# A decoder layer on one core: four score groups in one call over four banks, head and norm passes moved between engines, and the orders rewritten

## What is computed

```
x = layernorm(x + attn(x));  x = layernorm(x + wkv(x, ctx));  x = layernorm(x + ffn(x))

attn: q = rope(rms_norm(x@Wq.T + bq)) * gain     16 heads of 16 channels
      k = rope(rms_norm(x@Wk.T + bk)), v = x@Wv.T + bv      4 key heads, each shared by 4 query heads
      softmax(q k^T / 4, causal) v, then @Wo.T + bo
wkv:  num_t = exp(u + k_t) v_t + sum_{i<t} exp(k_i - (t-1-i) e^decay) v_i, den likewise without v, num / den
      with k = x and v = ctx, per channel
ffn:  (relu(x @ sign(up).T * up_s) @ sign(down).T) * down_s * out_s
```

## Time and profile before

| | |
|---|---|
| median of 3 runs | 215.16 us (214.39 to 215.67) |
| the profiled execution's own time | 215.18 us |
| its span, first to last instruction | 213.4 us |
| PE busy | 177.3 us (83%) |
| DVE busy | 177.4 us (83%) |
| ACT busy | 134.7 us (63%) |
| POOL busy | 114.2 us (54%) |
| mean granted TensorE clock | 0.964 |

### The profile page before, as it was taken

One profiled execution on the slowest core, in us unless ns is written; L12 is line 12 of the kernel. 1 busy time (PEld: TensorE's weight loads), 2 busy tenths in 40 slices (PEclk: granted clock), 3 DMA queues, 4 the chain that ended last, 5 costly groups with the idle time before them and its releaser, 6 DMA issues. The chain is left out here.

```text
span 213.4 us, 3906 instructions
## 1 busy us (share of the span) xinstructions
PE 177.3 (83%) x1240; PEld 106.4 (50%) x1240; DVE 177.4 (83%) x368; ACT 134.7 (63%) x250; POOL 114.2 (54%) x157
## 2 busy tenths in 40 slices
PE   1953897999999989999897999999799368689950
PEld 0432223354535745675375755746567347467740
DVE  2792555697996999999999999999999998998543
ACT  0443479957967789397478685778837329447820
POOL 7383247084176057835696369567255455376361
PEclk9999769999999999999999999999999999789995
DMA  6283915016600080033000530541010010010111
GB/s 216 51 309 134 260 61 123 5 27 136 185 0 2 3 221 0 3 66 108 5 0 0 120 104 0 146 129 49 2 54 0 0 49 3 2 49 0 52 52 52
DMA packets 19196, 14.81 MB, mean 69 GB/s; under 512 B 14307, under 2 KB 14563, under 8 KB 18918
## 3 DMA queue, kind: packets, MB, share of 16 engines
q1 hardware_dynamic: 18448, 14.43, 23.4%
q10 hardware_dynamic: 726, 0.11, 0.3%
HBM read 9.29 MB, written 2.10 MB: 53 GB/s over the span
## 5 line engine op out<-in xcount | busy, mean ns | idle before, releaser
L462 PE MATMUL banks<-dn_sb,hid_hi 128*128 128x256 bf16 x128 | 30.8, 281 | 8.2 <-DVE r L1517 4.7
L956 ACT ACTIVATE hid<-banks,ups_man 128x256 f32<-128x256 f32 x64 | 26.7, 473 | 14.9 <-PE banks L449 14.6
L903 ACT ACTIVATE probs<-banks 128x1024 f32<-128x1024 f32 x32 | 32.4, 1023 | 5.2 <-PE banks L359 5.0
L313 PE MATMUL banks<-wqkv_sb,xT_sb 128*128 128x384 f32 x64 | 26.4, 563 | 10.8 <-issue 6.2
L449 PE MATMUL banks<-x2hi,up_sb 128*128 128x256 f16 x128 | 29.6, 274 | 1.6 <-ACT hid L956 1.3
L462 PE MATMUL banks<-dn_sb,hid_lo 128*128 128x256 bf16 x128 | 30.7, 280 | 0.0
L449 PE MATMUL banks<-x2lo,up_sb 128*128 128x256 f16 x128 | 29.5, 273 | 0.0
L1226 POOL TENSOR_TENSOR newt<-ratio,rec 128x512 f32<-128x512 f32 x8 | 13.4, 1680 | 25.0 <-ACT rec L942 25.0
L313 PEld LDWEIGHTS banks<-wqkv_sb,xT_sb 128*128 128x128 f32 x64 | 13.1, 214 | 20.7 <-issue 13.1
L352 PE MATMUL banks<-rows 32*128 32x512 f16 x128 | 19.8, 386 | 2.6 <-ACT probs L903 1.2
L1594 DVE TENSOR_TENSOR hid_lo<-hid,hid_hi 128x512 f16<-128x512 f32 x24 | 19.0, 797 | 1.3 <-PE banks L462 1.1
(11 more groups left out here) (110 smaller groups left out, 382.3 us busy)
## 6 DMA issues: line engine op xcount, KB each, us to landing
xT_sb<-xT_dram SPq DMA_DIRECT2D x8, 256.0 KB, 3.2
x_sb<-x_dram SPq DMA_DIRECT2D x8, 256.0 KB, 3.3
ctxT_sb<-ctxT_dram SPq DMA_DIRECT2D x8, 256.0 KB, 3.5
out_dram<-outb SPq DMA_DIRECT2D x8, 256.0 KB, 2.2
up_f<-up_dram SPq DMA_DIRECT2D x1, 1024.0 KB, 4.9
dn_f<-down_dram SPq DMA_DIRECT2D x1, 1024.0 KB, 6.9
wqkv_sb<-wqkv_dram SPq DMA_DIRECT2D x1, 384.0 KB, 3.3
wo_sb<-wo_dram SPq DMA_DIRECT2D x1, 256.0 KB, 3.7
```

The lines of the kernel that those rows point to most:

```text
L313: nc.tensor.matmul(banks[:, PJ + t, 0:E], xT_sb[:, p % 2, c, t, :], wqkv_sb[:, c, :], start=(c == 0), stop=False)
L462: mm = nc.tensor.matmul(banks[:, DN, t * D:(t + 1) * D], part[:, j, t * S:(t + 1) * S], dn_sb[:, j, :], start=(j == 0 and t == 0 and m == ...
L903: nc.scalar.activation(probs[:, KVH * (m // 2) + m % 2:KVH * (m // 2) + m % 2 + 3:2].rearrange("p n j s -> p n (j s)"), banks[:, SC[m]:SC[ ...
L956: nc.scalar.activation(hid[:, j, :], banks[:, UP[n], (j % 2) * T * S:(j % 2 + 1) * T * S], ACT.Relu, scale=ups_man[:, j:j + 1]).then_inc(s ...
```

## The change

It has five parts.

1. `scores(p, t)` makes all four groups of a sequence in one call, over banks 6, 7, 2 and 3. The mask is added by products of 32 rows and 128 columns, four to a group. Half as many calls; `exps` still takes two banks at a time.
2. The banks are given out anew. Both products of a pair (`PV = (3, 2)`) share banks with the second half of a score call.
3. `normed(0, p)` and `normed(2, p)` run on ScalarE, as x * rstd + offset; GpSimd makes `less` = -mean and `offset` = less * rstd on two columns.
4. `scale_heads` and `keys_by_context` move from GpSimd to VectorE, with `newton_rms(1)`, `den_by_rec` of pairs 6 and 7 and `add_out` of pairs 0 and 7. `rope_sum` of pairs 1 to 7, `rope_sines(0)` and `rope_cosines(1)` move from VectorE to GpSimd, and of the 32 `low_bits` GpSimd has 16 (8 before).
5. The lists of TensorE, ScalarE, GpSimd and VectorE are in a new order; TensorE begins with seven products of zeros (`keep_busy`), and `project(2)` stands ahead of the branch. SP's list is the same.

```
-        PJ, AC, WO, X1, ZT, X2, DN = 2, 5, 0, 4, 2, 5, 0
-        PV = (1, 5)
-        UP = (5, 5, 0, 3)
-        SC = (6, 0, 6, 6)
+        PJ, AC, WO, X1, ZT, X2, DN = 4, 1, 1, 0, 4, 4, 1
+        PV = (3, 2)
+        UP = (4, 5, 3, 5)
+        SC = (6, 2, 6, 2)
+        NEWTON_ON_DVE = (1, )
...
+            def keep_busy(n):
+                pe.wait_ge(idle_ready, 1)
+                for k in range(n):
+                    nc.tensor.matmul(banks[:, X1], idle_b[:, 0:128], idle_b[:], start=True, stop=True)
...
+            def scores(p, t, guarded):
                 q = rows[:, p % 2]
                 landed(pe, "rows_in", p)
                 for k, kb in enumerate((HB * t + REP, T * HB + t)):
+                    for b in range(2):
+                        for s in range(2):
+                            r = VW * (b + 2 * s)
+                            nc.tensor.matmul(banks[:, SC[2 * t + b] + s], q[r:r + VW, kb, :],
+                                             q[r:r + VW, HB * t:HB * t + REP, :].rearrange("p j s -> p (j s)"),
+                                             start=(k == 0), stop=False)
+                for h in range(S // VW):
+                    for b in range(2):
+                        for s in range(2):
+                            r = VW * (b + 2 * s)
+                            mm[b][s] = nc.tensor.matmul(banks[:, SC[2 * t + b] + s]
+                                                        .rearrange("p (j s) -> p j s", j=REP)
+                                                        [:, :, h * VW:(h + 1) * VW],
+                                                        later[r:r + VW, h, :], masked[r:r + VW],
+                                                        start=False, stop=(h == S // VW - 1 and not guarded))
...
                 scores(0, 0, guarded)
-                scores(0, 1, guarded)
-                pe.wait_ge(sems["probs_done"], 1)
-                scores(0, 2, guarded)
                 pe.wait_ge(sems["probs_done"], 2)
+                scores(0, 1, guarded)
+                pe.wait_ge(sems["probs_done"], 4)
                 products(0, 0)
-                pe.wait_ge(sems["probs_done"], 3)
-                scores(0, 3, guarded)
+                pe.wait_ge(sems["probs_done"], 4)
+                products(0, 1)
...
+            def normed(n, p, rows_of, to, name):            # ScalarE
+                done(act, f"of{n + 1}", p)
...
+                for t in range(T):
+                    nc.scalar.activation(to[:, t], rows_of[:, t, :], ACT.Identity, bias=offset[n][:, t:t + 1],
+                                         scale=rstd[n][:, t:t + 1]).then_inc(sems[name], 1)
...
+                if n != 1:                                  # GpSimd, in with_eps
+                    nc.gpsimd.tensor_scalar(less[n][:], mv[n][:, :, 0], -1.0, 1.0, ALU.mult, ALU.mult)
...
+                if n != 1:                                  # GpSimd, in inverse_root
+                    nc.gpsimd.tensor_tensor(offset[n][:], less[n][:], rstd[n][:], ALU.mult)
```

More of the change, by code:

```diff
@@ L29 @@
 BR = 97
-HALF = S // 2
 HB = REP + 1
@@ L134, in build @@
         rstd = [sb(f"rstd{n}", [128, T]) for n in range(3)]
+        less = [sb(f"less{n}", [128, T]) for n in range(3)]
+        offset = [sb(f"offset{n}", [128, T]) for n in range(3)]
         ke = sb("ke", [128, NC, 2, T, SEG])
@@ new lines, in _ @@
+            normed(0, 0, r1, x1, "x1_done")
+            take_heads(3)
+            take_products(1, 0)
+            keys(0)
+            take_products(1, 1)
+            take_values(3)
+            squares(3)
+            signs()
+            first_guess(3)
+            take_channels(1)
+            exps(2, 0)
+            take_heads(4)
+            exps(2, 1)
+            log_den(0)
+            squares(4)
+            first_rec(0)
+            exps(2, 2)
+            exps(2, 3)
+            high_heads(3)
@@ L1235, in newton_rms @@
             def newton_rms(p):
+                k = p - sum(q < p for q in NEWTON_ON_DVE)
                 done(pool, "ssum_done", p)
@@ L1700, in _ @@
+            low_bits(0, 2)
+            moments(0, 3, r1)
+            refine(2)
             low_heads(5)
@@ L1758, in _ @@
-            num_by_rec(4)
-            attend_norm(6, 0)
-            moments(2, 1, r3)
             refine(4)
```

1059 lines of the change are left out of this document (530 added, 529 removed).

## The result

The changed kernel takes 209.37 us (209.04 to 209.37, 4 runs) against 215.18 us (214.39 to 215.67, 4 runs): ratio 0.9752, 95% interval 0.9706 to 0.9798. That is 5.8 us less; the forecast was 202.0, 13 us less. The direction and the range of 195 to 210 held, the size did not. The profiled execution took 209.36 us.

The account below looks back on a forecast made before the run. VectorE was taken to bound the middle, a latency chain the entry: first scan at 46, plus 139 of VectorE's work, 15.8 idle and 1.8 around it gave 202.6, stated as 202; range 195 to 210, forecast case 197 to 206.

Parts of the forecast that it names:

- the first scan at 46 us: End of the entry: the first scan starts at 46 us, 7 us earlier than the 52.9 of the kernel before.
- with idle time as before: Behind the first scan: VectorE idles 15.8 us, the same as in the kernel before.
- rival 2: Score calls: row groups overlap by two only, or masks pay a floor; a call takes 1.4 to 1.7; 207 us, chance 6%.
- TensorE, relieved of 14 us, doesn't take VectorE's place as the bound: Behind the first scan: TensorE loses 14 us and does not bound; its freed time can remove a few of 15.8 idle.
- a tail in which VectorE is mostly full until it drains: Last of three regimes of the kernel before: from 150 us on VectorE has 51.44 of 63.4 us busy.
- The first residual comes near 36: Entry: pair 0's attention ends earlier, so the first residual comes near 36 us, where it came at 46.0.
- Of these 10 us some 3 are lost again: From first residual to first scan: some 3 of 10 us gained are lost to ScalarE's queue and VectorE's pair 1 attention.
- they may run at the higher one for their second half and end at about 8: Entry: after idle products, the first eight projection products may reach TensorE's higher clock (2.4 GHz) and end at about 8 us.
- two calls with two exponentials of 1.03 each, 5.9 us: Entry: pair 0's scores and exponentials take 5.9 us, with no projection between scores and products.
- Rival 1: VectorE's queue: waiting for ScalarE's norms takes the place of saved work; only the entry's gain stays, 208 us; chance 17%.
- more than 10 us in total: Sign that the forecast is wrong: VectorE's waits for ScalarE or TensorE exceed 10 us in total.
- rival 3: VectorE and GpSimd's port: each moved subtraction costs VectorE 0.9 us, 7 of the 11 saved; 208 us, chance 8%.

Follow-up runs that it names:

- c1: The changed kernel without an edit, measured a second time against the kernel before: 207.74 us, ratio 0.9673.
- e10: The changed kernel with four extra products of 256 columns ahead of each of the 32 ffn_up calls: 212.95 us, ratio 0.9947 to the kernel before.
- e7: The changed kernel with sixteen extra products of 512 columns ahead of each score call: 215.08 us, ratio 0.9992 to the kernel before.
- e2: The changed kernel with each score call split inside, two row groups and then the other two: 209.53 us, ratio 0.9782 to the kernel before.
- e3: The changed kernel with the first and third norm's passes back on VectorE, without GpSimd's two tiny operations: 221.76 us, ratio 1.0346 to the kernel before.
- e11: The changed kernel with only the third norm's passes back on VectorE: 212.96 us, ratio 0.9968 to the kernel before.
- e6: The changed kernel with eight of GpSimd's sixteen low-bit subtractions back on VectorE: 210.51 us, ratio 0.9805 to the kernel before.
- e14: The kernel of e1 with the eight weight scalings moved from VectorE to ScalarE: 206.79 us, ratio 0.9641 to the kernel before the change.
- e5: The changed kernel with the eight key products back on GpSimd: 212.66 us, ratio 0.9922 to the kernel before.
- e1: The changed kernel with VectorE's small constants moved from ahead of head_sums(1) to behind swap_keys(1): 207.23 us, ratio 0.9674 to the kernel before.
- e13: The kernel of e1 measured again on the same chip as c1: 207.67 us, ratio 0.9662 to the kernel before the change.
- e8: The kernel of e1 with the very last norm pass, pair 7's third, on VectorE: 207.19 us, ratio 0.9651 to the kernel before the change.
- e4: The changed kernel without the seven idle products at TensorE's start: 208.60 us, ratio 0.9736 to the kernel before.
- e9: The changed kernel with VectorE's small constants later and without the seven idle products: 208.40 us, ratio 0.9743 to the kernel before.

## Why the prediction was right and its size was not

Between the scans the mechanism was right: VectorE bounds there, and TensorE, relieved, does not take its place. It was wrong for the tail, where VectorE's work was counted at full worth, and short for the entry. Two terms of the sum failed: the first scan at 46 us, which came at 49.7, and "with idle time as before", 15.8 us, which became 18.6. The sum was 46 + 139 + 15.8 + 1.8. The profile gives 49.7 + 139.2 + 18.6 + 1.9 = 209.4, that of c1 49.7 + 139.2 + 17.5 + 1.7 = 208.1. So the term of VectorE's work behind the first scan, on which most of the working was spent, is exact, though by offsetting errors; the two terms that were taken over or estimated are 3.7 and 2.8 us short (3.7 and 1.7 in c1).

*TensorE: right.* A call of 0.85 (0.77 at 92.0 us) for 0.86; rival 2 (two row groups at a time) is out. TensorE is busy 164.4, forecast 163. What the relief is worth is bounded by load added elsewhere: 9 us of it away from the scores cost 4 to 6 us (e10), some 14 ahead of them 5 to 7 (e7), and 5 us within the calls nothing that can be told (e2). "TensorE, relieved of 14 us, doesn't take VectorE's place as the bound" held.

*VectorE: right behind the first scan, not in all.* Busy 168.7 for 166, just above the prediction's own mark of 164 to 168. Behind the first scan it is 139.2 for 139: the key product cost 5.5 us for 6.6 and the numerators 7.9 for 6.6, two of them at 1.76 us. "7 of 8 rotation sums" is one too many (VectorE keeps those of pairs 0 and 7, so 4.9 us went and not 5.7). Ahead of the first scan VectorE worked 29.5 us where the forecast's figures leave 27; the six small constants alone took 3.6 us there for 1.0.

*The idle time: wrong.* The step was "With idle time as before: 46 + 139 + 15.8". Behind the last scan it rose from 10.6 to 12.0 us (12.1 in c1). The passes left VectorE there (1.8 us), and the tail shrank by 0.4: work taken off VectorE turned into its idle time. The reverse holds too: with 2.6 us given back to VectorE (e3, e11) the tail took 33.5 and 33.4 us. So VectorE's work is not the time of the tail; that a chain through ScalarE, GpSimd and TensorE is, is argued and not tested. The text said it itself ("a tail in which VectorE is mostly full until it drains") and then counted the tail's work at full worth. Between the scans the idle time rose from 5.2 to 6.6 us in the first profile and to 5.4 in c1; the difference is the wait behind pair 1's products at the lower clock (1.36 and 0.16 us). There the work counted nearly in full both ways: 3.7 us less of it than before the change gave 2.3 and 3.5, 5.0 more in e11 cost 3.9 to 5.1, and 2.4 more in e6 2.2 to 3.4. It counted less in e14, where 3.1 taken away gave 0.6 to 1.3, and not at all in e5, where 5.3 went to GpSimd with a handover ahead of each scan and the time rose by 1.4 to 2.6.

*The entry: the largest miss, 3.7 us.* "The first residual comes near 36" was 39.7, and "Of these 10 us some 3 are lost again" was right: 10.0 us from there to the scan. Of the 3.7 up to the residual, the DMA was 1.56 late (18.76 for 17.2), of which 0.82 is the slow projection that c1 did not have; c1 lost the same 0.82 again before the residual, at TensorE's lower clock. So "they may run at the higher one for their second half and end at about 8" is true of c1 (7.52) and not of the first profile (10.0). From the scores on 2.2 more are lost: the text gave "two calls with two exponentials of 1.03 each, 5.9 us", but from 22.64 to the products at 30.60 it is 8.0, because the exponentials stood 1.4 us behind `head_sums(1)` and its constants, and TensorE ran its second call and the products at the lower of the two clocks in part (tenths of 7, 5 and 7 from 20.8 to 36.3 us in the page's row): the second call took 1.47 us for 0.85, and from the products to the residual it was 9.1 us (10.0 in c1) for the 8.5 that were estimated. That ScalarE's queue would wait there was missed: the added wait was priced for the norms and not for the squares. How much it costs is open: single executions show 1.6 us (first exponentials at 22.7 in e1, 24.3 in c1), the medians of e13 and c1 nothing.

*ScalarE: mis-sized.* A pass takes 0.59 for 0.42; that met the prediction's own mark of "over 0.55 each". It is busy 149.3 for 148, because the rest of its groups sum to 3 us less, and it did not bound: TensorE's waits for exponentials total 8.9 us, below the 15 named. Rival 1 (waiting takes the place of the work) is near in its time, 208, and small in its mechanism: summed over the rows of the waits, VectorE waits 10.6 us for ScalarE and 8.1 for TensorE, before 6.8 and 7.0. That passes the mark of "more than 10 us in total", which the kernel before passed as well, so the mark told nothing. These waits grew by 4.9 us, and those for GpSimd fell by 6.6 (10.3 to 3.7).

*The port: rival 3 in part.* The eight `low_bits` moved to GpSimd are worth 1.1 to 2.8 us as they are (e6), so they did not cost what they saved; but 2.9 of their 5.5 us came back in VectorE's other operations, 0.36 us each where the rival had 0.9. By the Trainium skill, "SBUF — State Buffer", the section on the two separate sides, one of the two engines blocks for a whole instruction; the rows of `k_bias` (1.47 us for 0.17, ending with GpSimd's sum) and of the key copies in e13 agree. The mistake was to look for it in the large operations only.

*The shared banks: rival 4 out, but for a remainder.* TensorE waits 3.9 us in all for exponentials ahead of scores and 5.0 ahead of products. 2.65 of them stand ahead of pair 1's products, and the low granted clock that follows cost 1.2 us more in the first profile than in c1.

*What the gain is made of.* The two norms on ScalarE carry it: 13 to 14 us, 5 to 6 of them the third norm's (e3, e11). Without them the rest of the change is a loss of 3.5%. The key products on VectorE are worth 4 to 5 us although they load the fullest engine, the exchange of scaling and sum 2 to 4. The merged score calls were not taken back as such; by e10 and e7 the load that they save is worth some 4 to 6. These add up to more than the whole. The likely reasons are that the work that VectorE takes for its latency fits only since the norms have gone, and that the orders were written for all moves together (the 4.2 us of e3 ahead of the first scan are such a cost); neither is tested, since no run takes back two moves. No version tested is faster than the changed kernel by more than the runs can tell; the lowest medians are e14's 206.79 and e8's 207.19.

## What to carry to other kernels

Write the time as stages between the same event of the same loop (first and last scan here), and ask of each separately what an engine's microsecond is worth: here 0.6 to 1.4 us for each one added to VectorE at 95% between the scans or taken from it by the whole change, less for single moves off it (e14, e5), and nothing in the tail. Price every instruction that stands ahead of a critical one in its queue, however small, by what it takes beside GpSimd's long operations (`k_bias`, 1.47 us for 0.17). And measure the changed kernel a second time beside the edits: the first experiment's 2 us came from setting it against a single measurement, and the second one lay 1.6 us lower.

## What the runs showed of the hardware

- Operations of two columns are not short beside a busy neighbour: `k_bias` 1.47 us for 0.17, `less` 0.60 in the mean for 0.19 alone (at 202.73 us), `rstd` 0.91 in the mean for 0.70.
- ScalarE's pass with scale and bias from tiles, 256 columns from SBUF, takes 0.59 us, hardly less than its copy of 512 columns with 0.63.
- Four row groups of 32 run as one: eight products of 512 columns in 0.44 us and sixteen masks in 0.41. In the order of pairs (e2) TensorE still overlaps them across the pairs.
- The same sixteen products took 3.64 us at a granted clock of 0.50 and 1.92 at 1.00 (at 76.31 us).
- The first eight products behind the idle ones took 5.00 us in the first profile, behind a gap of 0.53 us, and 2.82 to 4.00 in the other thirteen, with gaps of up to 0.33; without the idle ones 4.32 and 4.94 (e4, e9). In the four fastest (2.82 to 2.88) the next eight took 4.46 to 4.54 us for 2.85.
